# Gathered tokens of a mixture-of-experts layer transposed by DMA in 16-bit halves instead of on TensorE

## The reference

```python
xn = _layernorm(x)                                   # (2, 512, 256)
x = x + attention(xn) + ffn(xn)

# ffn
logits = xf @ router_w.T + router_b
top_vals, top_idx = top_k(logits, 4)                 # 4 of 32 experts per token
rw = softmax(top_vals) * 1.8
g = silu(einsum('th,eih->tei', xf, gate_w))          # i = 192
u = einsum('th,eih->tei', xf, up_w)
routed = einsum('tei,ehi,te->th', g * u, down_w, combine)
shared = (silu(xf @ shared_gate_w.T) * (xf @ shared_up_w.T)) @ shared_down_w.T
```

## Time and profile before

| | before |
|---|---|
| median of runs | 200.52 us |
| profiled execution | 200.26 us |
| its span | 198.4 us |
| PE busy | 190.0 us (96%) |
| DVE busy | 117.5 us (59%) |
| ACT busy | 96.7 us (49%) |
| POOL busy | 111.8 us (56%) |
| DMA moved | 42.33 MB, mean 213 GB/s |

### The profile page before, as it was taken

One profiled execution on the slowest core, in us unless ns is written; L12 is line 12 of the kernel. 1 busy time (PEld: TensorE's weight loads), 2 busy tenths in 40 slices (PEclk: granted clock), 3 DMA queues, 4 the chain that ended last, 5 costly groups with the idle time before them and its releaser, 6 DMA issues.

```text
span 198.4 us, 4872 instructions
## 1 busy us (share of the span) xinstructions
PE 190.0 (96%) x1734; PEld 142.7 (72%) x1734; DVE 117.5 (59%) x360; ACT 96.7 (49%) x242; POOL 111.8 (56%) x156
## 2 busy tenths in 40 slices
PE   8998999999998899899999999999999999999994
PEld 2665756778565667698888678887867877687863
DVE  3478789898897766765632532433342144426894
ACT  3146248555889342653238647734934941123500
POOL 4133057525979468777777677777877743730000
PEclk9999999999999999999999999999999999999999
DMA  4994999998000029999975634324433335229963
GB/s 133 316 374 159 332 403 421 446 444 378 7 0 3 5 56 380 384 358 366 366 288 149 223 106 140 97 90 138 123 104 98 115 91 220 79 82 292 373 262 132
DMA packets 15000, 42.33 MB, mean 213 GB/s; under 512 B 2677, under 2 KB 6138, under 8 KB 14336
## 3 DMA queue, kind: packets, MB, share of 16 engines
q1 hardware_dynamic: 11376, 33.03, 45.5%
q0 software_dynamic: 3456, 8.92, 13.3%
q10 hardware_dynamic: 144, 0.07, 0.2%
HBM read 34.66 MB, written 7.86 MB: 214 GB/s over the span
## 4 chain that ended last, share of the span: by engine, by line
PE 73%; DMA 7%; DVE 7%; issue 4%; POOL 4%; ACT 3%; SPq 0%; ACTq 0%; POOLq 0%; DVEq 0%
PE bank L1575 20%; PE bank L1591 8%; PE bank L1783 5%; PE bank L1589 5%; DMA xg_mem<-xn_rows,codes 4%; PE bank L1440 4%; PE bank L1450 3%; PE bank L1553 3%; DMA w_mem<-w_qkvg_dram 3%; PE bank L1541 3%; PE bank L1612 3%; PE bank L1515 3%; DVE w_mem L1105 2%; PE bank L1465 2%; PE bank L1817 2%
## 5 line engine op out<-in xcount | busy, mean ns | idle before, releaser
L1575 PE MATMUL bank<-xb_mem,w_mem 128*128 128x128 f32 x384 | 47.7, 276 | 0.1
L1575 PEld LDWEIGHTS bank<-xb_mem,w_mem 128*128 128x128 f32 x384 | 45.4, 192 | 0.8 <-issue 0.3
L838 POOL DMA_INDIRECT y_rows<-y_mem,codes x36 | 36.2, 1007 | 16.8 <-issue 9.4
L830 POOL DMA_INDIRECT xg_mem<-xn_rows,codes x36 | 35.4, 984 | 13.0 <-issue 9.7
L1160 DVE TENSOR_TENSOR h_mem<-h_mem,bank 128x128 f32<-128x128 f32 x32 | 9.2, 287 | 42.2 <-ACT h_mem L641 41.9
L1105 DVE TENSOR_TENSOR w_mem<-bank,w_mem 128x512 f32<-128x512 f32 x32 | 20.1, 682 | 2.9 <-PE bank L1465 2.8
L640 ACT ACTIVATE h_mem<-bank 128x128 f32<-128x128 f32 x32 | 8.9, 277 | 23.5 <-PE bank L1575 23.1
L1168 DVE COPY y_mem<-bank 128x256 f32<-128x256 f32 x36 | 15.0, 424 | 7.3 <-PE bank L1591 4.5
L653 ACT COPY w_mem<-w_mem 128x1024 f32 x16 | 16.0, 1042 | 3.2 <-PE bank L1630 2.2
L1591 PE MATMUL bank<-w_mem,h_mem 128*128 128x256 f32 x60 | 17.0, 405 | 0.0
L1440 PE MATMUL bank<-w_mem 128*128 128x128 f32 x128 | 15.9, 278 | 0.2 <-DMA w_mem<-w_qkvg_dram 0.2
(11 more groups left out here) (168 smaller groups left out, 320.7 us busy)
## 6 DMA issues: line engine op xcount, KB each, us to landing
w_mem<-w_exp_dram SPq DMA_DIRECT2D x3, 3456.0 KB, 21.6
w_mem<-w_late_dram SPq DMA_DIRECT2D x7, 1152.0 KB, 8.1
w_mem<-y_rows SPq DMA_DIRECT2D x8, 512.0 KB, 7.3
w_mem<-w_qkvg_dram SPq DMA_DIRECT2D x2, 512.0 KB, 6.3
w_mem<-decay_dram SPq DMA_DIRECT2D x2, 512.0 KB, 7.6
xn_rows<-w_mem SPq DMA_DIRECT2D x2, 512.0 KB, 3.4
xnt_rows<-w_mem SPq DMA_DIRECT2D x1, 1024.0 KB, 4.9
w_mem<-w_ovf_dram SPq DMA_DIRECT2D x16, 64.0 KB
```

Source lines behind the costliest of these rows:

```text
L830: nc.gpsimd.indirect_dma_start(xg[:, k % RING, :], None, xn_rows, bass.IndirectOffsetOnAxis(ap=codes[:, c, 0:1], axis=0),).then_inc(tok_in ...
L838: nc.gpsimd.indirect_dma_start(y_rows, bass.IndirectOffsetOnAxis(ap=codes[:, c, 1:2], axis=0), ysb[:, k % YRING, :], None, bounds_check=RO ...
L1575: last = nc.tensor.matmul(ps_gu[j][:, m * P:(m + 1) * P], w[:, o:o + P], xbT[:, p % 2, (2 * g + j) * P:(2 * g + j + 1) * P], start=(g == 0 ...
```

## The change

Each normalised float32 token is also stored as two rows of 16-bit halves, all low halves and then all high halves: ACT copies the eight tiles into this order (`split_tokens`, in tiles 1 and 2 of attention, into the memory of `xg`), and SP stores them to a new DRAM tensor `xn_halves`, ahead of the third weight batch. The first writers of that memory after it (`hot_positions` on ACT and POOL) wait for the store.

From block 8 on (pair 4, and all overflow blocks) POOL gathers from `xn_halves`. SP transposes each gathered block by one DMA (`dma_start_transpose`, 128 x 512 elements of 16 bits) into `xp` (two pairs) or `xpO`, which lie in the memory of the shared weights. The low and high planes are joined to float32 by copies that write every second 16-bit element: for a pair's first expert and for overflow blocks by ACT, for the second expert by DVE, between its two multiplies of the step. PE has no transposes of tokens from pair 4 on. A gather waits for the transpose of the block that was in its slot.

SP issues the transposes after the late weights, in the order of the blocks; group 0 of the overflow weights stands behind overflow block 0, groups 1, 2 and 3 behind pairs 9, 12 and 15 (`OVER_BEHIND`), and the shared weights are loaded after the last join. Some semaphores are merged (`wo_in`, `tot_sb`).

```diff
+FIRST = RING // 2
+OVER_BEHIND = {O_BASE[j - 1] + 5: j for j in range(1, STATIC_O)}
...
                 if p + BATCH_IN == EARLY:
+                    sp.wait_ge(st_halves, NT)
+                    sp.dma_start(xn_halves.rearrange("(p t) c -> p t c", p=P),
+                                 xn_staged.rearrange("p t h d -> p t (h d)")).then_inc(halves_out, 16)
                     sp.wait_ge(xnT_ps, len(HEAD))
...
-            for j in range(STATIC_O):
+            def group_in(j):
                 experts = overflow_experts(SUBS * j)
                 if j == 0:
                     sp.wait_ge(we_in[PAIRS - 1], 16)
                     sp.wait_ge(res_sb, NT)
                 else:
                     sp.wait_ge(od_ps, j)
-                overflow_in(experts, wo_in[j])
-                if j == 0:
-                    sp.dma_start(ws_mem[:, :], w_shared).then_inc(ws_in, 16)
-            sp.wait_ge(xt_ps, len(X_ORDER))
+                overflow_in(experts, wo_in)
+            def transpose_block(k):
+                kind, n = SEQ_X[k]
+                sp.wait_ge(tok_in[k % RING], 16 * (k // RING + 1))
+                if kind == "O":
+                    if n >= 1:
+                        sp.wait_ge(xt_sb, X_AT["O", n - 1] + 1)
+                    sp.dma_start_transpose(xpO, xg_halves[:, k % RING, :]).then_inc(tpo_in, 16)
+                    return
+                p, j = n // 2, n % 2
+                if p >= FIRST + 2:
+                    if j == 0:
+                        sp.wait_ge(xt_sb, X_AT["P", 2 * (p - 2)] + 1)
+                    else:
+                        sp.wait_ge(xt2_sb, p - 2 - FIRST + 1)
+                sp.dma_start_transpose(xp[:, p % 2, j], xg_halves[:, k % RING, :]).then_inc(tp_in[p % 2][j], 16)
+            for k in range(2 * FIRST, len(SEQ_X)):
+                transpose_block(k)
+                kind, n = SEQ_X[k]
+                if (kind, n) == ("O", 0):
+                    group_in(0)
+                if kind == "P" and n % 2 == 1 and n // 2 in OVER_BEHIND:
+                    group_in(OVER_BEHIND[n // 2])
+            sp.wait_ge(xt_sb, len(X_ORDER))
+            sp.wait_ge(xt2_sb, PAIRS - FIRST)
+            sp.dma_start(ws_mem[:, :], w_shared).then_inc(ws_in, 16)
             sp.dma_start(xg_mem[:, :], xnt_rows).then_inc(xnt_in, 16)
...
+            def split_tokens(t):
+                act.wait_ge(xn_done, t + 1)
+                nc.scalar.copy(xn_staged[:, t], xn_split[:, t]).then_inc(st_halves, 1)
...
-                act.wait_ge(xt_ps, X_AT["P", 2 * p] + 1)
+                wait_transposed(act, p, 0)
                 need(act, gu_ps, 2 * (p - 1))
-                nc.scalar.copy(xbT[:, p % 2, :], ps_xt[p % 2][:, :]).then_inc(xt_sb, 1)
+                nc.scalar.copy(xbT_halves[:, p % 2, 0], xp[:, p % 2, 0].rearrange("p (h g) n -> p h g n", h=2)).then_inc(xt_sb, 1)
...
             def gather(k):
...
-                    pool.wait_ge(xt_ps, x_done(k - RING))
+                    wait_slot_read(pool, k - RING)
...
+            def take_pair_tokens(p):
+                wait_transposed(dve, p, 1)
+                need(dve, gu_ps, 2 * (p - 1))
+                nc.vector.tensor_copy(xbT_halves[:, p % 2, 1], xp[:, p % 2, 1].rearrange("p (h g) n -> p h g n", h=2)
+                                      ).then_inc(xt2_sb, 1)
...
             def expert_step(s):
                 if s < PAIRS:
                     multiply_unit(2 * s)
+                if FIRST <= s + 1 < PAIRS:
+                    take_pair_tokens(s + 1)
...
             def gate_up_overflow(j):
...
-                pe.wait_ge(wo_in[j], 16 * SUBS)
+                pe.wait_ge(wo_in, 16 * SUBS * (j + 1))
...
             def expert_step(s):
-                if 0 < s < PAIRS - 1:
+                if 0 < s < FIRST - 1:
                     transpose_pair(s + 1)
...
-                if s in O_BASE and s - 2 not in O_BASE:
-                    overflow_tokens(O_BASE.index(s))
```

More of the change, by code:

```diff
@@ L366, in build @@
         we_in = [sem(f"we_in{p}") for p in range(PAIRS)]
-        wo_in = [sem(f"wo_in{j}") for j in range(STATIC_O)]
+        wo_in = sem("wo_in")
         ones_sb = sem("ones_sb")
@@ L386, in build @@
         xt_sb = sem("xt_sb")
+        xt2_sb = sem("xt2_sb")
+        st_halves = sem("st_halves")
+        halves_out = sem("halves_out")
+        tp_in = [[sem(f"tp_in{a}{j}") for j in range(2)] for a in range(2)]
+        tpo_in = sem("tpo_in")
         gu_ps = sem("gu_ps")
@@ L418, in build @@
         diag_sb = sem("diag_sb")
-        tot_sb = [sem(f"tot_sb{i}") for i in range(NT - len(PE_TILES))]
+        tot_sb = sem("tot_sb")
         block = ctx.enter_context(nc.Block())
@@ L453, in down_bank, with whole_rows, wait_slot_read, wait_transposed @@
             return ps_dn[j][:, 0:D] if p < PAIRS - 1 else ps_sd[1][j][:, 0:D]
-        def x_done(k):
+        def whole_rows(k):
+            return k < 2 * FIRST
+        def wait_slot_read(eng, k):
             kind, n = SEQ_X[k]
-            return X_AT[kind, n - n % 2 if kind == "P" else n] + 1
+            if whole_rows(k):
+                eng.wait_ge(xt_ps, X_AT["P", n - n % 2] + 1)
+            elif kind == "P":
+                wait_transposed(eng, n // 2, n % 2)
+            else:
+                eng.wait_ge(tpo_in, 16 * (n + 1))
+        def wait_transposed(eng, p, j):
+            eng.wait_ge(tp_in[p % 2][j], 16 * ((p - FIRST) // 2 + 1))
         @block.sync
@@ L710, in _ @@
                     take_features(3)
+                if t in (1, 2):
+                    split_tokens(4 * t - 4)
+                    split_tokens(4 * t - 3)
                 if t >= 2:
@@ L714, in _ @@
                 take_values_gate(t + 1)
+                if t in (1, 2):
+                    split_tokens(4 * t - 2)
+                    split_tokens(4 * t - 1)
                 hot_positions(t, "vg")
@@ L1564, in gate_up @@
                 p, j = n // 2, n % 2
-                pe.wait_ge(xt_sb, X_AT["P", 2 * p] + 1)
+                if p < FIRST or j == 0:
+                    pe.wait_ge(xt_sb, X_AT["P", 2 * p] + 1)
+                else:
+                    pe.wait_ge(xt2_sb, p - FIRST + 1)
                 need(pe, h_sb, 2 * (n - 1))
@@ L1684, in expert_step @@
                     down_overflow(O_BASE.index(s - 2))
-                if s in O_BASE and s - 2 in O_BASE:
-                    overflow_tokens(O_BASE.index(s))
                 if s - 1 in O_BASE:
@@ L1896 @@
     xn_rows = nc.dram_tensor("xn_rows", (TOK, D), F32, kind="Internal").ap()
+    xn_halves = nc.dram_tensor("xn_halves", (TOK, 2 * D), U16, kind="Internal").ap()
     xnt_rows = nc.dram_tensor("xnt_rows", (P, KT * TOK), F32, kind="Internal").ap()
     y_rows = nc.dram_tensor("y_rows", (ROWS, D), F32, kind="Internal").ap()
-    build(nc, *args, xn_rows, xnt_rows, y_rows, out)
+    build(nc, *args, xn_rows, xn_halves, xnt_rows, y_rows, out)
     r = run_bass_kernel_spmd(nc, [{n + "_dram": v for n, v in arrays.items()}], core_ids=[0])
```

37 lines of the change are left out of this document (26 added, 11 removed).

## The result

The changed kernel takes **216.82 us** (median of four runs, 215.90 to 218.84); the kernel before, run beside it on the same chip, 200.42 (199.93 to 200.70). The ratio is 1.0835, with an interval of 1.0754 to 1.0916. The prediction said slower, and 208.2 with a range up to 214.0: the direction was right, the size not. The profiled execution took 217.16 us, its span is 215.2 us, 16.8 more than before.

The account below looks back on a forecast made before the run. PE, which never rests, and nearly full POOL were taken to bound the kernel side by side. Overflow 3's late weights +6.7, pair 15's transposes -0.4, slow restart +1.5 gave +7.8 on 200.26: 208.1, forecast 208.2 us, range 203.8 to 214.

Parts of the forecast that it names:

- Removed work: PE's transposes of pairs 4 to 15 and four overflow blocks: 6.2 us off PE's path at most, about 3%.
- Early stage, joins, tail: ACT's early copies and extra store, low/high joins on ACT and DVE, shared weights loaded late: all counted as hidden, 0.
- First late place: Pair 4: first transpose lands behind late weights at 103.5, PE stands 2.6 us, POOL stays 1.7 us late.
- slow restart: PE's matmuls after the stand at overflow 3 run slower at first: 1.5 us lost, ends 0 and 3.
- Ring order: SP's queue at pair 4: descriptors taken in ring order, so the first transpose lands at 103.5 or later, not about 98.
- Overflows 1 and 2: Their weights, behind pairs 9 and 12, take back PE's gain and little more; overflow 2 at 146.4 against 145.23.
- Second late place: Overflow 3's weights, issued behind the last gather and pair 15's transposes: gate_up_overflow starts at 164.6, not 157.86, +6.7 us.
- The sum: +6.7 - 0.4 + 1.5 = +7.8 on the profiled 200.26: 208.1 for that execution, 208.2 as forecast.
- signs named for being right: PE idle 2 to 3 us near 102, 5 or more near 160; last weight issues after 159; last gather 154 to 156.
- The transposes themselves are the bound: Rival: 28 blocks on one queue set the pace above 2.2 us each; 211 us, or 281 at 5 each; chance 0.12.
- Only the second stall: Rival: transposes pass the weights, so pair 4 costs POOL nothing and only overflow 3 stalls; 204.9 us; chance 0.2.
- Faster: Rival: PE's 6.2 us come off if overflow 3's weights land by 157; 194.1 us, 197 with half; chance 0.06.

Follow-up runs that it names:

- k_quarter: Kernel before the change, with 36 of 48 PE transposes left out and nothing in their place: 197.49 us, ratio 0.9862.
- w_keep_on: Changed kernel, with matmuls nobody reads put on PE ahead of pair 4 and overflows 1 and 3: 215.61 us, ratio 1.0735.
- h2: Changed kernel, with overflow weight groups 1 and 2 behind overflow blocks 1 and 2, group 3 behind pair 14, numbers read ahead: 209.15 us.
- e4: Kernel before the change, with overflow weight groups 1 to 3 read and issued only after pairs 9, 12, 15 are gathered; no DMA transposes: 207.44 us.
- h4: Changed kernel with DMA transposes from pair 7 and overflow block 1, weight groups 1 to 3 behind overflow blocks 1 to 3, numbers read ahead: 199.55 us, ratio 0.9954.
- g1: Changed kernel, with overflow weight groups 1 to 3 behind pairs 8, 11, 14 and expert numbers read a pair earlier: 212.85 us, ratio 1.0597.
- g3: Changed kernel with g1's move, plus transposes of blocks 8 to 12 ahead of the last late weight load and group 0 behind pair 6: 214.03 us.
- h5: h4 with ACT copying overflow 3's weights ahead of its join of that overflow block: 200.04 us, ratio 0.9907.

## Why the prediction was wrong

- **Removed work.** At most 6.2 us, and worth nearly its full size where nothing else is in the way (k_quarter: 3.04 of 3.96). Right.
- **Early stage, joins, tail.** Early: 0, as counted; +0.4 us at expert 5 is within the scatter of the kernels that share this stage. The extra store landed at 46.9, not by 45, and ACT's first write behind it began at 47.0 instead of 46.63. ACT's join takes 0.76 us, not the 0.58 of the copy that it replaces, DVE's 0.44, not 0.6. The tail: 0, as counted; in the chain of waits the shared stage starts at 190.89 and the span ends 24.3 us later, as before (198.4 - 174.07 = 24.3).
- **First late place: the place was right, the size not. This is the step that failed:** "POOL is 2.2 us late and had 0.47 us to give at 110.26, so 1.7 us stay". POOL was 4.6 us late at scatter 4 and 6.0 at the one after 110. Three terms were missing. The block landed at 105.1 and not at 103.5, since it is itself work behind the weights (issued at 94.97, it took 10.1 us, against the median of 3.1). PE's 24 matmuls behind the stand ran at half pace, 5.25 us for 2.84; a slow restart was counted only for the second stall. And the transposes stood behind each other: with all five in the queue by 104.3, ACT could join the first at 105.1 and overflow block 0 at 110.5. That block, ACT's weight copies and the silu behind them would have been late even without the slow restart (w_keep_on).
- **Ring order.** The Trainium skill ("DMA: Bandwidth & Descriptors", "Queues, rings and completion order") says that an engine takes a queue's descriptors in ring order, though a later one may finish first; the prediction read it as: the transposes land behind the weights. The trace agrees: the last load, issued at 94.55, landed 9.3 us later, at 103.9, and the first transpose at 105.1.
- **Overflows 1 and 2: the second failed step.** "They take back what PE has gained by then, and little more" was worked out for POOL 1.7 us late. Overflow 1 cost 4.7 us in the table. Its chain has the same steps as the one written for overflow 3 and took longer than its sum, 13.6 us (from the gather at 123.06 to PE at 136.63) against 9.7; and it began 6 us late, behind pair 4. With groups 1 and 2 placed earlier (h2) the loss is gone.
- **Second late place.** Right in place and nearly in size: from the last gather's start to gate_up_overflow(3) it took 11.1 us (162.48 to 173.62) against 9.7; the transpose's issue took 1.2 for 0.6, the four reads 2.8 for 2.3 (166.63 to 169.43). e4 shows that 5.3 of the 6.5 us come from the order alone. The 1.5 us for the restart there was 1.3 (2.79 less 1.50), but that is luck: it was read from matmuls at the start, with the granted clock at 1.00, and what came is the lower level of the clock, 0.53.
- **The sum.** The last gather is 7.6 us later than forecast (162.48 for 154.9), the chain behind it 1.4 longer; what follows, 17.3 us to the shared stage (190.89 - 173.62), is as forecast (16.2 - 0.4 + 1.5). That is 9.0 of the 9.06 us between 208.1 and 217.16. Of the signs named for being right, the late issues (169.43) and the stand of over 5 us (6.24) came; the first stand was 4.9 us, not 2 to 3, and the last gather at 162.5, not 154 to 156.
- **The rivals.** "The transposes themselves are the bound" is refuted as priced: where they queue they take 1.36 us a block, under the 2.2 from which they would set the pace, and with 21 of the 28 blocks still on DMA h4 is not slower than the kernel before. The Trainium skill's figure ("VectorE: DVE Perf Modes", "The three transpose paths") gave an estimate of 5.2 us for four 128x128 pieces in a row; the trace of w_keep_on shows 1.36 us for a whole block of 128x512, and the measurement decides. "Only the second stall" fell with pair 4's landing: the transposes did not pass the weights. "Faster" needed overflow 3's weights in place, where the prediction put it, but not them alone: g1 has them there and took 212.85. The sign changes, by 0.5%, in h4, where pair 4's and the other groups' places are right as well.

## What to carry to other kernels

When work moves to a DMA queue, write down that queue's list in order of time, with what each entry waits for, and put every entry ahead of any that waits for something later than its own use: here four places mattered, and in g1 to g3 moving one entry made another late. Price a late start by the engine that has no slack behind it and by all that stands in its in-order list (here ACT: join, weight copies, silu), not by the first waiter alone. And ask what is left when all waits are gone: DMA transposes from pair 7 on, in the best orders found, gain 0.5% (h4) to 0.9% (h5), where the plain removal of less PE work gave 1.4%.

## What the runs showed of the hardware

- PE ran at half pace behind stands of 3.8 to 6.2 us (granted clock 0.51 to 0.59 there), and at full pace, clock 1.00, when matmuls that nobody reads filled the stand (2.92 instead of 5.25 us). Behind a stand of 1.83 us it ran at full pace (1.50). Stands between came out either way: twelve matmuls of 1.5 us took 2.43 behind 2.29 us (g3) and 2.90 behind 2.42 (w_keep_on), but 1.58 behind 2.82 (g1).
- A transpose of 128x512 16-bit elements took SP 1.2 us to issue, against 0.6 for a 64 KB load, and landed 3.1 us after its issue (median). SP's queue carried 26,752 packets instead of 11,376 (the 1 MB store's among them); of all packets 17,925 were under 512 bytes, before 2,677.
- A copy of 128x512 16-bit elements into every second place took 0.76 us on ACT and 0.44 on DVE.
